# Keys for mixing loaded and rotated with keys on the partitions, in place of turning the rotated ones on TensorE

## The reference

```
q_big  = einsum(hidden_q, Wq, w_kc_q) with rotary tables      # carried to 128 values per head before this stage
kv_r   = kv_c * cos_k + rotate_half(kv_c) * sin_k             # rotated keys, 257 x 128 per batch row
scores = einsum('bhsr,bhlr->bhsl', q_r, k_r)
attn   = softmax(scores, axis=-1)
ctx_c  = einsum('bhsl,bld->bhsd', attn, kv_r)                 # the mixing: the same rotated keys serve as values
out    = x + (ctx_c carried through w_kc_kv and Wo)
```

## Time and profile before

| | us |
|---|---|
| median of 3 runs | 1603.02 (1601.88 to 1604.45) |
| the profiled execution | 1603.56 |
| its span, first to last instruction | 1601.4 |
| the crossing within the span | about 461 to 968 |

### The profile page before, as it was taken

One profiled execution on the slowest core, in us unless ns is written; L12 is line 12 of the kernel. 1 busy time (PEld: TensorE's weight loads), 2 busy tenths in 40 slices (PEclk: granted clock), 3 DMA queues, 4 the chain that ended last, 5 costly groups with the idle time before them and its releaser, 6 DMA issues. The chain is left out here.

```text
span 1601.4 us, 26509 instructions
## 1 busy us (share of the span) xinstructions
PE 1485.5 (93%) x8136; PEld 1123.1 (70%) x8136; DVE 1139.9 (71%) x1820; ACT 811.1 (51%) x1739; POOL 541.8 (34%) x594
## 2 busy tenths in 40 slices
PE   4799999999978999999999977999898899999997
PEld 3577777777746777777777766888443478787876
DVE  6888777887648788788788853777687735556466
ACT  4566565666545555555555543555211355554554
POOL 4244333442025554544545513221351202222021
PEclk9899999999989999999999988999898899999999
DMA  4223334243565444544544514000244100000000
GB/s 152 68 81 111 105 110 119 75 122 95 182 219 126 119 119 105 125 111 106 129 107 108 139 21 172 0 0 0 84 174 158 45 1 1 27 1 26 0 27 27
DMA packets 140917, 140.05 MB, mean 87 GB/s; under 512 B 84150, under 2 KB 111926, under 8 KB 139708
## 3 DMA queue, kind: packets, MB, share of 16 engines
q1 hardware_dynamic: 140284, 138.54, 30.0%
q10 hardware_dynamic: 576, 0.81, 0.2%
HBM read 109.88 MB, written 27.39 MB: 86 GB/s over the span
## 5 line engine op out<-in xcount | busy, mean ns | idle before, releaser
L997 ACT ACTIVATE c_e<-c_sc_ps,c_peak 128x257 f32<-128x257 f32 x256 | 119.6, 473 | 219.4 <-DVE c_peak L900 219.4
L878 POOL TENSOR_TENSOR c_mixed_low<-c_whole,c_mixed_high 128x512 fp32r<-128x512 f32 x64 | 81.9, 1279 | 211.0 <-ACT c_mixed_high L1017 211.0
L77 DVE TENSOR_TENSOR b_rot_parts_low<-b_rot,b_rot_parts_high 128x1536 fp32r<-128x1536 f32 x64 | 136.0, 2125 | 21.9 <-ACT b_rot_parts_high L541 21.9
L278 POOL TENSOR_TENSOR b_turned_raw<-b_turn_part 128x384 f32<-128x384 f32 x32 | 70.1, 2190 | 166.2 <-DVE b_key_parts_low L77 165.0
L1571 PE MATMUL f_ps<-f_right,f_left 128*128 128x512 f32 x256 | 115.7, 613 | 8.4 <-ACT f_raw L1614 6.1
L70 PE MATMUL c_out_ps<-c_shared_high,c_mixed_high 128*128 128x512 f32 x256 | 112.2, 438 | 11.1 <-issue 10.1
L324 DVE TENSOR_TENSOR b_rot<-b_w_qr,b_angle 128x1536 f32<-128x1536 f32 x64 | 119.2, 1862 | 0.2
L70 PE MATMUL b_ps<-c_shared_high,b_wq_parts_high 128*128 128x512 f32 x256 | 108.5, 424 | 6.5 <-DVE c_shared_low L77 6.5
L70 PE MATMUL e_mm_ps<-folded_high,e_h_t_high 128*128 128x512 f32 x256 | 106.4, 416 | 5.7 <-DVE e_h_t_low L77 5.6
L541 ACT ACTIVATE b_rot_parts_high<-b_rot 128x1536 fp32r<-128x1536 f32 x64 | 95.3, 1489 | 24.5 <-PE b_ps L72 17.0
L274 POOL TENSOR_TENSOR b_turn_part<-b_early,b_centre 128x384 f32<-128x384 f32 x64 | 82.1, 1303 | 72.2 <-DMA b_early<-early 70.5
(11 more groups left out here) (232 smaller groups left out, 3903.8 us busy)
## 6 DMA issues: line engine op xcount, KB each, us to landing
c_ends_spread<-end_weights SPq DMA_DIRECT2D x64, 256.0 KB, 4.3
carried_queries<-x SPq DMA_DIRECT2D x7, 2048.0 KB, 11.3
b_early<-early SPq DMA_DIRECT2D x15, 640.0 KB, 4.0
f_left<-ent_in SPq DMA_DIRECT2D x16, 512.0 KB, 5.4
f_right<-ent_out SPq DMA_DIRECT2D x16, 512.0 KB, 6.5
c_q_first<-carried_queries SPq DMA_DIRECT2D x32, 224.0 KB, 3.3
c_q<-carried_queries SPq DMA_DIRECT2D x32, 224.0 KB, 3.2
b_late<-late SPq DMA_DIRECT2D x16, 320.0 KB, 3.8
```

Source lines behind the costliest of these rows:

```text
L77: return nc.vector.tensor_tensor(low, value, high.bitcast(F32), ALU.subtract)
L878: nc.gpsimd.tensor_tensor(mixed[1][:, w, :, u], whole[:, u % 2].rearrange("p (h s) -> p h s", h=H), mixed[0][:, w, :, u].bitcast(F32), ALU ...
L997: last = nc.scalar.activation(e[:, v, c], sc_ps[:, 2 * v + c, 0:L], ACT.Exp, bias=peak[:, v, c:c + 1], accum_out=total[:, v, c:c + 1])
```

## The change

The keys that `mix` needs are no longer made by turning the rotated keys on TensorE. They are loaded a second time from a second input, `cache_n`, in which the 256 keys lie on the partitions (two blocks of 128 keys, 1 KB per partition, 128 KB per batch row), and rotated on GpSimd by a table `rope_n` of the same shape.

- SyncE: one load of the table, and per batch row `load_own`, two rows ahead of its use in a pair of buffers. In the tile loop it stands first in each batch row's part, behind a wait for `own_chained`, that is for the two products of the batch row two before.
- GpSimd: `rotate_own`, two batch rows ahead, in the second half's step behind `keep_ends`: two products of 256 elements and two half sums of 128. The first two batch rows are done ahead of the loop.
- TensorE: `turn_kv` goes, with its bank of PSUM.
- ScalarE and VectorE: `round_kv` and `split_kv` read the new keys in SBUF, one batch row earlier than before, the first ahead of the loop.
- The new table, loads, products and keys lie in `spare[:, 0:2048]`. So at the end SyncE issues `spread_ends` of the last tile's first batch row, waits for the last `split_kv`, and only then loads the next stage's weights into `spare`; the three other `spread_ends` stand behind that.

```diff
+        own = spare[:, 0:2048].rearrange("p (n k d) -> p n k d", n=8, k=2)
+        own_table, own_raw, own_part, own_kv = own[:, 0:2], [own[:, 2 + v] for v in range(2)], own[:, 4:6], [own[:, 6 + v] for v in range(2)]
...
-        kv_ps = ctx.enter_context(nc.psum_tensor("c_kv_ps", [P, D], F32))
...
+            def load_own(b, u):
+                sp.dma_start(own_raw[u % 2], cache_n[bass.ds(b, 1)].rearrange("b p k d -> p (b k) d")).then_inc(own_loaded[u % 2], 16)
+
             def tile(i, w):
                 for u in range(BT):
                     b = BT * i + u
+                    if not (isinstance(b, int) and b < 2):
+                        wait(sp, own_chained, 2 * (b - 2) + 2)
+                        load_own(b, u)
                     if known(i, 1):
                         wait(sp, rotated_, b - BT + 1)
                         crossing.load(sp, b, u)
...
+            sp.dma_start(own_table, rope_n).then_inc(own_table_loaded, 16)
+            for u in range(2):
+                load_own(u, u)
             for u in range(2, BT):
                 crossing.load(sp, u, u)
             in_tiles(sp, tile)
+            spread_ends(TILES - 1, 0)
+            sp.wait_ge(kv_split, B)
             holo.load(sp, holo_loaded)
-            for u in range(BT):
+            for u in range(1, BT):
                 spread_ends(TILES - 1, u)
...
+            def rotate_own(b, u, t):
+
+                half = DC // 2
+                pool.wait_ge(own_loaded[u % 2], 32 * t + 16 * (u // 2) + 16)
+                wait(pool, own_ready, 2 * b)
+                nc.gpsimd.tensor_tensor(own_part[:, 0], own_raw[u % 2], own_table[:, 0], ALU.mult).then_inc(own_chained, 1)
+                nc.gpsimd.tensor_tensor(own_part[:, 1], own_raw[u % 2], own_table[:, 1], ALU.mult).then_inc(own_chained, 1)
+                pool.wait_ge(own_chained, 2 * b + 2)
+                wait(pool, kv_split, b - 1)
+                for lo, hi in ((0, half), (half, 0)):
+                    nc.gpsimd.tensor_tensor(own_kv[u % 2][:, :, lo:lo + half], own_part[:, 0, :, lo:lo + half], own_part[:, 1, :, hi:hi + half],
+                                            ALU.add).then_inc(own_ready, 1)
...
             rotate(1, 1, 0)
+            pool.wait_ge(own_table_loaded, 16)
+            for u in range(2):
+                rotate_own(u, u, 0)
...
                     keep_ends(n, i, u, half)
                     if half == 0 and not (isinstance(b, int) and b + 2 >= B):
                         rotate(b + 2, (u + 2) % BT, i + (u + 2) // BT)
+                    if half == 1 and not (isinstance(b, int) and b + 2 >= B):
+                        rotate_own(b + 2, (u + 2) % BT, i + (u + 2) // BT)
                     if half == 1 and (u or known(i, 1)):
                         split_mixed(b - 1, (u - 1) % BT, w if u else 1 - w)
...
-                low_part(nc, kv[1][:, u], kv_ps[:, 0:2 * P].rearrange("p (k x) -> p k x", k=2), kv[0][:, u]).then_inc(kv_split, 1)
+                low_part(nc, kv[1][:, u], own_kv[u % 2], kv[0][:, u]).then_inc(kv_split, 1)
...
-                    if half == 0:
-                        split_kv(b, u)
+                    if half == 0 and not (isinstance(b, int) and b + 1 >= B):
+                        split_kv(b + 1, (u + 1) % BT)
...
             find_peak(0, 0)
             normalise(0, 0)
+            split_kv(0, 0)
             in_tiles(dve, tile)
...
             def round_kv(b, u):
-                act.wait_ge(kv_turned, b + 1)
+                act.wait_ge(own_ready, 2 * b + 2)
                 wait(act, mix_done, b - BT + 1)
-                nc.scalar.activation(kv[0][:, u], kv_ps[:, 0:2 * P].rearrange("p (k x) -> p k x", k=2), ACT.Copy).then_inc(kv_rounded, 1)
+                nc.scalar.activation(kv[0][:, u], own_kv[u % 2], ACT.Copy).then_inc(kv_rounded, 1)
...
-            def turn_kv(b, u):
-                pe.wait_ge(rotated_, b + 1)
-                wait(pe, kv_split, b)
-                for k in range(2):
-                    last = nc.tensor.transpose(kv_ps[:, k * P:(k + 1) * P], kv_t[u][:, k * P:(k + 1) * P], ident[:])
-                last.then_inc(kv_turned, 1)
...
                     turn_weights(n, half)
-                    if half == 0:
-                        turn_kv(b, u)
```

More of the change, by code:

```diff
@@ L737, in first, with cross_attention @@
             self.load(sp, u, u)
-def cross_attention(nc, crossing, holo, x, q_dram, w_vo_dram, ends_dram, x1, stat, ident, eps, half_pi, left_counted):
+def cross_attention(nc, crossing, holo, x, cache_n, rope_n, q_dram, w_vo_dram, ends_dram, x1, spare, stat, ident, eps, half_pi, left_counted):
     with ExitStack() as ctx:
@@ L779, in cross_attention @@
         out_ps = ctx.enter_context(nc.psum_tensor("c_out_ps", [P, D], F32))
-        kv_ps = ctx.enter_context(nc.psum_tensor("c_kv_ps", [P, D], F32))
         x_loaded = sem("c_x_loaded")
         q_loaded, rotated_, pool_chained = crossing.q_loaded, crossing.rotated, crossing.pool_chained
-        kv_turned, kv_rounded, kv_split = (sem(f"c_{n}") for n in ("kv_turned", "kv_rounded", "kv_split"))
+        own_table_loaded, own_chained, own_ready, kv_rounded, kv_split = (
+            sem(f"c_{n}") for n in ("own_table_loaded", "own_chained", "own_ready", "kv_rounded", "kv_split"))
+        own_loaded = [sem(f"c_own_loaded{v}") for v in range(2)]
         scored, peaked, exped, normed = sem("c_scored"), sem("c_peaked"), sem("c_exped"), sem("c_normed")
@@ L863, in rotate @@
                 wait(pool, scored, 2 * (b - BT) + 2)
-                wait(pool, kv_turned, b - BT + 1)
                 wait(pool, mix_taken, b - BT + 1)
@@ L1032, in tile @@
                     round_turned(n, b, u, half)
-                    if half == 0:
-                        round_kv(b, u)
+                    if half == 0 and not (isinstance(b, int) and b + 1 >= B):
+                        round_kv(b + 1, (u + 1) % BT)
                     if half == 1 and (u or known(i, 1)):
@@ L1041, in _ @@
             exponential(0, 0)
+            round_kv(0, 0)
             in_tiles(act, tile)
@@ L2047, in _, with perceiver_block @@
             add_row(TURNS - 1, G - 1)
-def perceiver_block(nc, x, x_s, cache_t, early, w_qr, w_kr, late, angle_q, centre_q, rope_kv, amp_nat, phase_nat, basis_t, basis_o, amp_o, phase_o,
+def perceiver_block(nc, x, x_s, cache_t, cache_n, rope_n, early, w_qr, w_kr, late, angle_q, centre_q, rope_kv, amp_nat, phase_nat, basis_t, basis_o, amp_o, phase_o,
                     ent_in, ent_out, path, columns, rows, gate_w, gate_b, out):
@@ L2078, in perceiver_block @@
             left_counted = range(min(used), max(used) + 1)
-            cross_attention(nc, crossing, holo, x, q_dram, w_vo_dram, ends_dram, x1, stat, ident, eps, half_pi, left_counted)
+            cross_attention(nc, crossing, holo, x, cache_n, rope_n, q_dram, w_vo_dram, ends_dram, x1, spare, stat, ident, eps, half_pi, left_counted)
         folded = [ctx.enter_context(nc.sbuf_tensor(f"folded_{part}", [P, 4, CD, D], F32R)) for part in ("high", "low")]
@@ L2116 @@
     rope_kv = np.stack([cos_k.T, (sin_k * sign_k).T], axis=1)
+    by_key = lambda a: a[:, :L - 1].reshape(len(a), 2, P, DC).transpose(0, 2, 1, 3)
     rows = lambda a, c: a.reshape(H, c, P, -1).transpose(0, 2, 1, 3).reshape(H, P, -1)
@@ L2136 @@
         "x": g["x"].reshape(B * S, D), "x_s": g["x"].transpose(1, 0, 2).reshape(B * S, D), "cache_t": g["ctx_512"].transpose(0, 2, 1),
+        "cache_n": by_key(g["ctx_512"]), "rope_n": by_key(np.stack([cos_k, np.roll(sin_k * sign_k, DC // 2, axis=1)])).transpose(1, 0, 2, 3),
         "early": early, "w_qr": rows(g["xattn_W_qr"], CQ), "w_kr": g["xattn_W_kr"].transpose(0, 2, 1).reshape(H // 2, P, DC), "late": late,
```

## The result

The changed kernel takes 1704.89 us, the median of 4 runs (1702.62 to 1706.00), against 1602.99 for the kernel before (4 runs, 1601.88 to 1604.45): a ratio of 1.0633, 95% interval 1.0615 to 1.0652. It is slower by 102 us. The profiled execution took 1706.0 us with a span of 1703.9, so 102.5 us more span than before. The forecast was 1698.

What follows compares the result with a forecast made beforehand. The prediction took the end weights' DRAM round trip, a two-row loop through SyncE's queue, to bound the changed kernel: 1603.6 + 80 (loop) + 3 (start) + 11 (tail) = 1698 us, range 1655 to 1740.

Steps and rivals of the forecast that it cites:

- The deciding step: SyncE's queue: the `own_chained` wait puts loads ahead of the store, 5.2 us later against 2.9 us of room.
- The sum of the delay, 5.53: From the start of `keep_ends` to the store on SyncE's queue: 5.53 us in place of 0.36.
- The +80: Crossing's loop over sixty rows: 30 loops of 17.48 us, 524 less 444.6, so +80 us.
- by 1 to 2.5 us in nearly each row: Sign of being right: VectorE's `add_end` stands idle for a DMA by that much in nearly each row.
- The lower bound: Whole kernel: low end of the forecast's bounds, loop 16.4 us, +47, with the ends 1661 us.
- The start: Stage opening: GpSimd rotates two rows of own keys ahead of its first `keep_ends`: +3 us (1 to 5).
- partly in that idle time: Stage opening: two GpSimd passes of 2.4 us fall partly in the 2.56 us idle before the first `keep_ends`.
- The tail: Stage end: row 61's `spread_ends` stands behind the next stage's weight loads, delaying `add_end`: +11 us (7 to 13).
- TensorE's 16 us: Two transposes per row removed from TensorE: 0.25 x 64 = 16 us at most, vanishing in the longer loop.
- the first rival: At `add_end`: the round trip stays hidden, so not slower: 1602, or 1588 if the ends cost nothing; 7%.
- The second rival: GpSimd and VectorE share SBUF access, lengthening VectorE's products and splits: 35 us, about 1635; 6%.
- The third rival: TensorE's clock falls in new gaps of some 1.5 us a row: +270 us, near 1870; 3%.

Runs made afterwards that it cites:

- the first two experiments: Changed kernel with SyncE's wait for `own_chained` and own-key load moved behind `spread_ends`: 1618.01 us; changed kernel with four own-key buffers, the wait looking back four rows: 1617.11 us.
- the tail mended: Four-buffer kernel with `own_part` and `own_kv` in their own SBUF and row 61 spread ahead of the next stage's loads: 1607.26 us.
- the loop mended: Changed kernel with the store freed by moving the wait behind it (1618.01 us) or by four own-key buffers (1617.11 us, or 1607.26 with the end-of-stage change).
- the version with the split moved: Four-buffer kernel with its end-of-stage delay removed, plus own keys rounded ahead of the exponentials and split right behind `find_peak`: 1605.19 us.
- the late store alone: Kernel before with one added wait: SyncE waits for `keep_ends` ahead of its raw key loads, with no added work or load: 1620.65 us.
- the wait for the sums: Changed kernel with SyncE waiting for `own_ready`, the half sums of `rotate_own`, in place of `own_chained`, its products: 1726.35 us.

## Why the prediction was right

**The deciding step held.** That a zero of idleness ahead of `add_end` hid some room (2.9 us in the row read, 2.2 on average over rows 2 to 57), that the new wait puts the key and query loads between `keep_ends` and the store, and that the loop returns after two rows: all three stand in the rows of after, and the first two experiments give back 87 and 88 us when only the wait ahead of the store is changed. The sum of the delay, 5.53, was made of spacings of the earlier trace rows and measured 5.67. The pieces behind it nearly cancelled their errors: the wait from store to spread is 2.1 and not 1.5, the landing 3.7 and not 4.3. The +80 became +86; of the 6 missing, 4 are the pace over rows 2 to 57 (0.06 x 60), the rest the first and last rows, where single loops are longer. The sign "by 1 to 2.5 us in nearly each row" held on average only: 34 rows lie in it, 8 above, and 14 wait less than 0.3. The lower bound's own terms add up to 1659 and not 1661, which changes nothing.

**The start was under-sized:** +5.5 where I had +3 (1 to 5). The step that failed is "partly in that idle time". GpSimd's first own product and the crossing's first `keep_ends`:

```profile
467.12 0.73 POOL L888 TENSOR_TENSOR spare<-spare 128x256 f32<-128x256 f32 x1 [2.80 <-DMA spare<-cache_n]
...
472.11 0.19 POOL L901 TENSOR_TENSOR c_ends<-c_e,c_inverse 128x2 f32<-128x2 f32 x1
```

The load lands at 467.12, later than `keep_ends` ran in before (465.70), so none of the two passes hides in the idle time: 1.4 for the load and 5.0 for the two passes, 6.4 us there, of which 5.5 are left one row on.

**The tail held** at +11.5 against 11, by the mechanism named; that the sizes agree so closely is partly luck. The last split of VectorE, the first of the next stage's loads, row 61's spread, and its `add_end`:

```profile
1019.07 0.41 DVE L77 TENSOR_TENSOR c_kv_low<-spare,c_kv_high 128x256 fp32r<-128x256 f32 x1
...
1019.52 0.34 SPq L676 DMA_DIRECT2D spare<-phase_nat  x1
...
1026.52 0.33 SPq L829 DMA_DIRECT2D c_ends_spread<-end_weights  x1
...
1030.37 1.12 DVE L957 SCALAR_TENSOR_TENSOR c_whole<-c_ends_spread,c_kv_t,c_mix_ps 128x512 f32<-128x512 f32 x1 [9.95 <-DMA c_ends_spread<-end_weights]
```

From the first load to the spread it took 7.0 us, not 8.6: the 8.6 held a wait for `keep_ends` of row 60, which ended at 912.71, behind the last load (issued by 911.45). So `add_end` of row 61, counted from its own `keep_ends`, came 9.8 us later than before, not 11.6. The other 1.6 came at rows 62 and 63, which the prediction did not count.

**TensorE's 16 us** did vanish in the loop, as said. But the first rival's price, 1602 "or down to 1588", was wrong: with the round trip hidden the kernel takes 1617 to 1618, and with the tail mended 1607. The step that failed is the gain of up to 16 us in it: the pace with the loop mended was 7.37 to 7.39 against 7.41, 1 to 3 us in 60 rows. The earlier trace rows had a hint: part of TensorE's idle time ahead of its turns was a wait for VectorE, so TensorE's share of 97.6% did not prove that its work was what a row costs. The experiments above say what takes the gain back only in part.

**The second rival,** shared access, did not show in after: the median of `normalise` is 697 ns against 696 in the earlier trace rows, and the mean 744 against 765; that VectorE's work falls into other gaps when it waits for the landing is the likely reason, not tried. It showed as soon as the loop was mended (median 822, mean 826), as the prediction put it, hidden behind the loop. Its price of 35 us was too high: taking GpSimd's products away won 5.7, of which 4.3 lie in the 60 rows of the loop. The splits did not lengthen in the changed kernel (median 408 ns in both); only the version with the split moved shows what the prediction feared for them.

**The third rival,** TensorE's clock, came in a small part. The granted clock in after, over most of the loop (columns as above):

```profile
493.00:1010.00 517.00, 424.19 (x1965) 336.04 (x1964) 344.91 (x652) 240.67 (x733) 364.80 (x588) 0.96 0.45 112
```

So the reading "such short gaps do not do it" was too strong, while the rival's price, all matmuls at the lower level, stayed far off. What the slow stretches cost was not tried by itself. That they set the pace is unlikely: the piece of the loop in which work on the engines stands, `add_end` to `keep_ends` of two rows on, is 5.91 us against 6.20 in before, and the loop's growth is the delay of the store.

## What to carry to other kernels

When a transfer stands on a queue that serves in order, a new wait on that queue costs what everything behind it loses: write down for each wait what is queued behind it, who needs that, and how much room it has. An idle time of zero ahead of an instruction does not say how far its data was ahead; the room is read from the order of time. And where the busiest engine waits for others that are busy four fifths of the time, as here, work taken from it can be worth little, and nothing if it is added to one of them: look first for idle time on the engine that it waits for, into which existing work can be moved, and at what runs beside it there.

## What the runs showed of the hardware

- The time from the store to the landed spread stayed between 5.5 and 6.3 us: 1.79 + 4.26 = 6.05 us in before, 5.84 in after, 5.52 with the late store alone, 5.62 with the wait for the sums, and 5.9 to 6.3 in the others. Where the store comes 3.5 us or more after `keep_ends`, behind the loads, the landing took 3.6 to 3.7 us; where it comes early, 3.8 to 4.3. So in these runs a part of a delay ahead of the store was given back. The reason was not tried.
- Where instructions of GpSimd and VectorE with both inputs in SBUF ran at the same time, the one that started later nearly waited for the other. In the version with the split moved, the split took 885 ns and not 409 beside a `split_mixed` that stayed at 1.28 us (1270 to 1280 ns on average): in all 55 rows from 500 to 900 us it started later, and its time followed what was left of `split_mixed` (0.42 to 0.77 us) one for one, with 0.28 us more. GpSimd's product went from 693 to 1135 ns where it started while a normalising product ran. Moving an instruction into an engine's idle time can therefore cost a good part of what it fills.
